# One table of places per body: the order of all stages of a deformable-convolution and mixture-of-experts block laid anew

## The reference

```python
def conv(u):                                    # u = ln_c(x)
    x_proj = u @ w_in + b_in
    x1 = gelu(ln(depthwise3x3(u) + dw_bias) * ln_gamma + ln_beta)
    offset = (x1 @ w_off + b_off)               # 8 groups, 9 taps, 2 coordinates
    mask = softmax(x1 @ w_mask + b_mask)        # over the 9 taps of a group
    # every tap reads x_proj at its shifted place, between four neighbours
    samp = bilinear_gather(pad(x_proj), px, py)
    return sum_over_taps(samp * mask) @ w_out + b_out

def ffn(t):                                     # t = ln_t(x), 8 experts, 64 -> 256 -> 64
    probs = softmax(xt @ Wr + br); top_p, top_idx = top_k(probs, 2)
    y[e] = gelu((xn * ln_g[e] + ln_b[e]) @ W1[e] + b1[e]) @ W2[e] + b2[e]
    return sum of the two chosen experts, weighted by top_p / top_p.sum()

x = x + conv(ln_c(x));  x = x + ffn(ln_t(x))
```

## Time and profile before

| what | value |
|---|---|
| median of 3 runs | 313.14 us (313.05 to 313.84) |
| the profiled execution's own time | 313.73 us |
| its span in the trace | 311.9 us |
| PE, ACT, DVE, POOL busy in the span | 280.0, 257.3, 231.8, 121.9 us |
| prologue | 0 to 29.03 us |
| first, second, third, last body | 59.64, 68.30, 67.29 us, and from 224.26 us on |

### The profile page before, as it was taken

One profiled execution on the slowest core, in us unless ns is written; L12 is line 12 of the kernel. 1 busy time (PEld: TensorE's weight loads), 2 busy tenths in 40 slices (PEclk: granted clock), 3 DMA queues, 4 the chain that ended last, 5 costly groups with the idle time before them and its releaser, 6 DMA issues.

```text
span 311.9 us, 8480 instructions
## 1 busy us (share of the span) xinstructions
PE 280.0 (90%) x3312; PEld 180.5 (58%) x3312; DVE 231.8 (74%) x658; ACT 257.3 (82%) x495; POOL 121.9 (39%) x123
## 2 busy tenths in 40 slices
PE   8977998959899998899999997999978999998895
PEld 3552566626567654445667663444767787776462
DVE  6999679998957967579778876498958244479355
ACT  3888679897896999989796999988868899888473
POOL 5230151504452705031583413050966713569230
PEclk9999999997999999999999999999999999999999
DMA  6910000000000000000000000000000000000000
GB/s 151 300 37 0 3 3 3 3 0 0 2 3 2 3 3 0 2 0 3 2 8 14 0 2 2 1 2 0 2 20 0 3 2 2 11 0 12 2 1 17
DMA packets 7189, 4.84 MB, mean 16 GB/s; under 512 B 5089, under 2 KB 6830, under 8 KB 7086
## 3 DMA queue, kind: packets, MB, share of 16 engines
q1 hardware_dynamic: 7150, 4.31, 5.6%
HBM read 2.04 MB, written 0.52 MB: 8 GB/s over the span
## 4 chain that ended last, share of the span: by engine, by line
PE 42%; DVE 22%; ACT 18%; issue 9%; POOL 7%; DMA 1%; DVEq 0%; ACTq 0%; POOLq 0%
ACT wk L1279 5%; PE zl_ps L1528 4%; ACT wk L1274 4%; PE ga_ps L1559 3%; PE m_ps L1661 3%; PE zh_ps L1525 3%; PE ga_ps L1561 3%; PE ga_ps L1560 3%; DVE wx L849 3%; DVE prod L861 3%; PE m_ps L1644 2%; ACT h_all L1310 2%; PE m_ps L1502 2%; DVE samp L876 2%; POOL prod L546 2%
## 5 line engine op out<-in xcount | busy, mean ns | idle before, releaser
L861 DVE TENSOR_TENSOR prod<-ga_ps,wx 128x480 f32<-128x480 f32 x96 | 61.9, 651 | 36.5 <-PE ga_ps L1561 35.8
L1274 ACT ACTIVATE wk<-zh_ps 128x512 f16<-128x512 f32 x108 | 65.4, 605 | 22.3 <-PE zh_ps L1525 21.3
L546 POOL TENSOR_TENSOR prod<-prod 128x960 f32<-128x960 f32 (+1 forms) x20 | 39.7, 1986 | 112.0 <-DVE prod L861 112.0
L1559 PE MATMUL ga_ps<-v_all,wk 128*128 128x80 f16 x576 | 79.8, 202 | 2.4 <-DVE prod L861 1.6
L1561 PE MATMUL ga_ps<-v_all,wk 128*128 128x80 f16 x576 | 79.8, 202 | 0.0
L1560 PE MATMUL ga_ps<-v_all,wk 128*128 128x80 f16 x576 | 79.8, 202 | 0.0
L1559 PEld LDWEIGHTS ga_ps<-v_all,wk 128*128 128x128 f16 x576 | 56.9, 99 | 15.5 <-issue 7.6
L1279 ACT ACTIVATE wk<-zl_ps 128x512 f16<-128x512 f32 x108 | 65.6, 607 | 0.1
L1560 PEld LDWEIGHTS ga_ps<-v_all,wk 128*128 128x128 f16 x576 | 57.4, 100 | 8.2 <-issue 0.5
L1561 PEld LDWEIGHTS ga_ps<-v_all,wk 128*128 128x128 f16 x576 | 57.6, 100 | 0.0
L1528 PE MATMUL zl_ps<-tab,sel_lo 128*128 128x512 f16 x108 | 42.1, 390 | 7.0 <-ACT wk L1279 4.4
(11 more groups left out here) (283 smaller groups left out, 610.9 us busy)
## 6 DMA issues: line engine op xcount, KB each, us to landing
v_all<-still SPq DMA_DIRECT2D x1, 1440.0 KB, 10.4
h_all<-in_W SPq DMA_DIRECT2D x1, 512.0 KB
w_s<-in_W SPq DMA_DIRECT2D x1, 512.0 KB
x_tok<-in_x SPq DMA_DIRECT2D x1, 384.0 KB, 6.5
out_dram<-x_tok SPq DMA_DIRECT2D x6, 64.0 KB, 1.8
w_high<-w_high SPq DMA_DIRECT2D x1, 256.0 KB, 2.9
const<-in_table SPq DMA_DIRECT2D x1, 218.0 KB, 2.7
vec<-in_vectors SPq DMA_DIRECT2D x1, 132.5 KB
```

The lines of the kernel that those rows point to most:

```text
L546: then(pool.tensor_tensor(p[:, 0:3, :], p[:, 0:3, :], p[:, 3:6, :], ALU.add))
L861: dve.tensor_tensor(prod[q % 2][:].rearrange("p k n -> p (k n)")[:, f * PB * NV:(f + 1) * PB * NV] .rearrange("p (n c l) -> p n c l", n=PB ...
L1274: act.activation(wk[n % WR][:, 0, :], zh_ps[:], ACT.Relu, scale=W_SCALE).then_inc(s_wkh, 1)
L1559: pe.matmul(to, w_h, high, start=True, stop=False)
```

## The change

Nothing but the tables at the head of the module differs. `MIDDLE` is replaced by `SECOND` and `THIRD`, and all the tables are written out with new numbers. The lists of bodies then read:

```diff
-PE_AT = [PE_FIRST] + [PE_MIDDLE] * (CHUNKS - 2) + [PE_LAST]
+PE_AT = [PE_FIRST, PE_SECOND, PE_THIRD, PE_LAST]
...
-POOL_LAST = {"tap_tree": [4, 22.5, 29.5, 44, 45.5, 56.5, 67, 71.5], "combine": [34, 63.5], "conv_rstd": 30.5,
-             "inner_rstd": 0, "input_rstd": 47, "half_inner_rstd": 46, "router_exp": 22, "half_router_exp": 66}
+POOL_LAST = {"tap_tree": [1, 14, 26.5, 34, 37.5, 47.5, 54.5, 67.5], "combine": [28.5, 71], "conv_rstd": 31, "inner_rstd": 0,
+             "input_rstd": 3, "half_inner_rstd": 45, "router_exp": 15, "half_router_exp": 54}
```

More of the change, by code:

```diff
@@ L51 @@
 TINY = 2.0 ** -120
[L55 to L95, removed]
+PE_FIRST = {"input_t": 3.5, "convolve": [7, 8.5, 9, 9.5], "project": 6.5, "image_t": [10, 11.5], "conv_t": 14.5, "offsets":
+            15.5, "table": [23, 27], "samples_t": 12, "project_out": 8, "experts_t": 12.5, "router": 10, "expert_in": [10,
+            20, 26.5, 44.5, 47.5, 54, 56.5, 71, 74, 92.5, 101, 105.5, 108.5, 112, 113.5, 122], "expert_out": [11.5, 11.5,
+            13.5, 17, 19, 20.5, 23, 24], "outputs_t": [17, 25.5], "b2": 15, "bias_product": [0, 0, 0, 0, 4.5, 4.5, 4.5, 5.5],
+            "zeros": [19.5, 22.5, 19.5]}
@@ new lines @@
+ACT_FIRST = {"pad_image": 3.5, "project_high": 7.5, "image_out": 10.5, "conv_gelu": 14.5, "tap_exp": 18.5, "distances": [21,
+             21, 22, 22, 23], "samples_out": 6, "zn_out": 17, "router_exp": 8, "hidden": [6, 18, 24, 35, 35.5, 40, 47.5, 52,
+             60.5, 66.5, 69.5, 76, 76, 76.5, 77, 82.5], "outputs_out": [31.5, 31]}
+DVE_FIRST = {"input_stats": 13.5, "input_norm": 29, "input_low": 2.5, "conv_stats": 8.5, "project_low": 7, "conv_norm": 10.5,
+             "image_out": 10.5, "positions": [14.5, 17, 16.5], "rows": [17.5, 19.5, 20.5, 22], "edges": 15, "hats": 25,
+             "tap_weights": [22, 25], "lane_sum": [9.5, 9.5, 17.5, 17.5, 27, 28, 0, 3], "residual": 4.5, "inner_norm": 12,
+             "zn_low": 2, "route": [4, 13, 14.5], "expert_weights": 14.5, "b2": 14, "bias_rows": 5, "router_parts": 0,
+             "w1_low": [6.5, 10.5, 13, 25.5], "outputs_in": [17.5, 9.5], "second_stats_": 0, "second_norm": 0}
@@ new lines @@
+POOL_FIRST = {"tap_tree": [8, 10, 16.5, 29.5], "combine": [0.5, 21], "conv_rstd": 9, "inner_rstd": 4.5, "input_rstd": 19.5}
+PE_SECOND = {"input_t": 1, "convolve": [5, 5.5, 6, 7], "project": 4.5, "image_t": [11.5, 13.5], "conv_t": 14, "offsets": 15,
+             "table": [34.5, 35.5], "samples_t": 3, "project_out": 4.5, "experts_t": 10, "router": 12, "expert_in": [11.5,
+             13, 13.5, 13.5, 16, 17, 18.5, 18.5, 19, 19, 22.5, 23, 24, 25, 27, 28], "expert_out": [17.5, 22, 26, 31.5],
+             "outputs_t": [34.5, 35.5], "b2": 9.5}
@@ new lines @@
+PE_THIRD = {"input_t": 1, "convolve": [5.5, 6.5, 7.5, 8.5], "project": 4.5, "image_t": [9.5, 12.5], "conv_t": 14, "offsets":
+            15.5, "table": [33.5, 35.5], "samples_t": 3, "project_out": 4.5, "experts_t": 8, "router": 11.5, "expert_in":
+            [12, 13, 13.5, 14, 16.5, 16.5, 18.5, 19, 20.5, 21, 22.5, 23, 24.5, 25, 27, 28], "expert_out": [18, 22, 26.5,
+            31.5], "outputs_t": [33.5, 34], "b2": 21}
+ACT_SECOND = {"pad_image": 1.5, "project_high": 5.5, "image_out": 11.5, "conv_gelu": 14.5, "tap_exp": 16.5, "distances":
+              [19.5, 20, 20.5, 21.5, 21.5], "samples_out": 3.5, "zn_out": 10.5, "router_exp": 15.5, "hidden": [12.5, 12.5,
+              15, 15, 17.5, 18, 18.5, 18.5, 21.5, 22, 23, 23.5, 26, 26.5, 27.5, 28.5], "outputs_out": [19.5, 24.5, 30.5,
+              33.5]}
@@ new lines @@
+POOL_SECOND = {"tap_tree": [13, 20, 21, 25], "combine": [28.5, 35.5], "conv_rstd": 16, "inner_rstd": 11, "input_rstd": 19.5}
+POOL_THIRD = {"tap_tree": [19, 22, 25.5, 26.5], "combine": [32.5, 32.5], "conv_rstd": 13.5, "inner_rstd": 9, "input_rstd": 0}
+PE_LAST = {"input_t": 7.5, "convolve": [4.5, 9, 15.5, 21], "project": 0, "image_t": [11.5, 25], "conv_t": 24.5, "offsets":
+           13.5, "table": [37, 27], "samples_t": 3.5, "project_out": 5.5, "experts_t": 11, "router": 15, "expert_in": [17.5,
+           19.5, 20, 22, 24.5, 27.5, 29, 29, 31.5, 35, 36, 36.5, 40.5, 40.5, 43.5, 46], "expert_out": [22.5, 26, 32, 32,
+           44.5, 44.5, 47, 48], "outputs_t": [34.5, 55.5], "b2": 25, "half_samples_t": 48.5, "half_project_out": 50.5,
+           "half_experts_t": 57, "half_router": 61.5, "zeros": [5.5, 11]}
```

31 lines of the change are left out of this document (24 added, 7 removed).

## The result

The changed kernel takes 310.67 us (median of seven runs, 310.53 to 312.25) against 313.14 us (313.05 to 313.84). The ratio is 0.9926 with a 95% interval of 0.9903 to 0.9948: 2.5 us faster, 310.8 was forecast. The profiled execution took 310.67 us, with a span of 308.9. In some runs of most of these kernels, the one before included (313.74 to 315.95 against 313.05 to 313.24), the granted clock of PE falls for a while and the time is longer; where a median mixes both, "at full clock" names the runs without it.

The account below looks back on a forecast made before the run. No single engine bounds it: PE and ACT feed each other place by place. Terms 0 + 0.5 - 1.4 - 0.6 - 0.8 = -2.3 take the profiled 313.73 to 311.4, less 0.6 for the median: 310.8 us, range 307.5 to 314.0.

Parts of the forecast that it names:

- Third body, -1.4: Third body: ACT's waits in the first half fall from 3.6 us to 2.2, between 0 and -2.5.
- `project_high`: Third body, place 7.5: this ACT work beside a group of convolution removes ACT's wait of 0.97 us.
- the spread distances: Third body, places 20.5 to 24.5: ACT gets work beside two long products, so a 0.4 us wait goes.
- Second body, +0.5: Second body: positions -0.45, long product +0.45, `outputs_t` +0.5, together +0.5 us, between -1 and +1.5.
- `expert_out` without its cover: Second body, place 22: the long PE product comes after most of ACT's distances, so ACT waits, +0.45 us.
- `outputs_t` behind the tables: Second body: both bursts stand behind the next chunk's tables, +0.5 us, between 0 and 1.04.
- rival B: Waits only move and both middle bodies come out at 0: 312.3 or 313.1 us, chance 0.21.
- Seam, -0.6: Third body to last: `wx` ahead of fill 21 misses the tap tree, `lane_sum` starts earlier, -0.6 us, between 0 and -1.6.
- Tail, -0.8: End of last body: `combine` moves into POOL's gap and the last tree ends earlier, -0.8 us, between 0 and -0.9.
- what is left of the chain moves with it: Tail: everything after the last tap tree comes earlier along with the tree's end, -0.8 us.
- C: Slower: DVE stages waiting for input hold weighings, PE's gathers and ACT; 315.0 to 316.9 us, chance 0.17.
- A: Bigger gain: all 6.9 us of ACT's first-half waits in both middle bodies go, 304.8 us, chance 0.12.

## Why the prediction was right, point by point

The time was right to 0.1 us, and that closeness is luck: the third body gave 0.5 more than forecast and the tail 0.5 less. Most terms held, but not each for its reason.

- **Third body, -1.4.** ACT's waits in the first half went from 3.6 to 2.23 us, as worked out (2.2). What was missed is 0.4 in the second half and some 0.1 in single instructions, so the body gave 1.9. The step's reason was half right. The opening itself gave 2.88 - 2.23 = 0.65, and the spread of `convolve` is what it hangs on (0.8 in time, shown); `project_high` is worth not 0.97 but 0.16 (shown). The other 0.72 are the waits of 0.42 at 178.55 and 0.30 at 184.09. The prediction gave the 0.42 to the spread distances, and that step is wrong: the distances stand behind it, at 195.28 before, and it is gone without their spread, too. In the changed kernel a `wk` lies between the two `hidden` (12.5 and 13 for twice 12.5); that this takes the wait was not run by itself.
- **Second body, +0.5.** It came to +0.28, out of terms most of which were wrong. Ahead of `expert_out` ACT's waits fell by 3.3 - 2.2 = 1.1 where I had 0, probably since PE's groups are spread there too. `expert_out` without its cover cost 0.45, as taken. `outputs_t` behind the tables cost the body itself nothing. Not seen at all: longer waits in the second half, 0.51, 1.02 and 1.55 us for 0.39, 0.77 and 0.97, where by the tables ACT's outputs moved away from beside the expert products; no run shows that cause by itself. ACT waits 6.57 us in this body before and after: here the waits only moved, which is rival B in one body. ACT's timeline after:

```profile
132.82 0.60 ACT L1283 ACTIVATE wk<-zh_ps 128x512 f16<-128x512 f32 x1 [0.51 <-PE zh_ps L1534]
...
140.52 0.60 ACT L1283 ACTIVATE wk<-zh_ps 128x512 f16<-128x512 f32 x1 [1.02 <-PE zh_ps L1534]
...
148.73 0.60 ACT L1283 ACTIVATE wk<-zh_ps 128x512 f16<-128x512 f32 x1 [1.55 <-PE zh_ps L1534]
```

- **Seam, -0.6.** Held, and with its reason: `wx` is short once the tree can't meet it; 0.54 in the trace, 0.56 by itself.
- **Tail, -0.8.** The step that failed is "what is left of the chain moves with it". The last tree did end 0.90 earlier, as worked out, but DVE's sums gained only 0.65 of it, and PE stood next with some 0.3 us to give: -0.3. The spare time for `combine` was there (POOL idles 1.32 us before `y_r`). The Trainium skill, page "SBUF — State Buffer", section "Who interferes with whom", has VectorE in a two-port mode and GpSimd shut each other out; the collision of `y_ve` with `combine` that was feared by it did not arise, since `y_ve` at 290.05 lay well behind `combine`'s end at 288.96; the rule is not tested there.
- **Rivals.** B is what happened in the second body and not in the third. C did not happen in the changed kernel, but its mechanism is real and its price, 1.9 us in one body (shown), lay inside the range given. A did not happen: of 6.9 us that ACT waits in the two first halves, 2.1 went. More of it could be had: with THIRD in both bodies, and two stages of the second moved, the time is 309.02.
